# Where the first attention's keys are expanded, and when the gated layer's gates are copied

## What is computed

```python
x = x + tanh(g_xattn[0]) * retention(layernorm(x), ctx)      # decaying sum of k*v
x = x + tanh(g_ffn[0])   * moe(layernorm(x), 8 experts, top 2, gelu, hidden 512)
x = x + tanh(g_xattn[1]) * attention(layernorm(x), ctx)      # 16 heads of 8, rope, softmax
x = x + tanh(g_ffn[1])   * moe(layernorm(x), 8 experts, top 2, silu(a) * b, hidden 352)
x = x + tanh(g_xattn[2]) * additive attention(layernorm(x), ctx)   # tanh over all pairs
x = x + tanh(g_ffn[2])   * moe(layernorm(x), 16 experts, top 4, silu(a) * b, hidden 128)
x = x + tanh(g_xattn[3]) * attention(layernorm(x), ctx)
x = x + tanh(g_ffn[3])   * moe(layernorm(x), 8 routed experts and a shared one, top 2, gelu)
```

## Time and profile before

| | us |
|---|---|
| median of 3 runs | 616.18 (615.16 to 616.81) |
| the profiled execution | 613.41 |
| its span, first to last instruction | 611.6 |
| TensorE busy | 563.5 (92%) |
| VectorE busy | 445.4 (73%) |
| ScalarE busy | 415.8 (68%) |
| GpSimd busy | 117.0 (19%) |

### The profile page before, as it was taken

One profiled execution on the slowest core, in us unless ns is written; L12 is line 12 of the kernel. 1 busy time (PEld: TensorE's weight loads), 2 busy tenths in 40 slices (PEclk: granted clock), 3 DMA queues, 4 the chain that ended last, 5 costly groups with the idle time before them and its releaser, 6 DMA issues.

```text
span 611.6 us, 8766 instructions
## 1 busy us (share of the span) xinstructions
PE 563.5 (92%) x3281; PEld 390.9 (64%) x3284; DVE 445.4 (73%) x684; ACT 415.8 (68%) x581; POOL 117.0 (19%) x74
## 2 busy tenths in 40 slices
PE   7999999978998999998865899999998999999997
PEld 5667887846776777776210247556655777788886
DVE  4358988768646889986968658576767836787786
ACT  4779888916754565656999976624504856988885
POOL 5400000241210000002999914200000310000000
PEclk9999999979999999999899999999999999999999
DMA  6207110200200811020000022604610110812100
GB/s 233 70 15 298 49 55 1 73 2 1 75 1 3 312 38 41 34 69 1 2 5 1 1 69 70 194 16 122 190 34 1 38 36 0 297 50 70 35 1 34
DMA packets 16782, 40.27 MB, mean 66 GB/s; under 512 B 1834, under 2 KB 6058, under 8 KB 16740
## 3 DMA queue, kind: packets, MB, share of 16 engines
q1 hardware_dynamic: 16740, 39.71, 19.5%
HBM read 39.01 MB, written 0.70 MB: 65 GB/s over the span
## 4 chain that ended last, share of the span: by engine, by line
PE 71%; DVE 13%; ACT 11%; issue 3%; POOL 1%; ACTq 0%; DVEq 0%; POOLq 0%
PE ps L680 38%; ACT work L1046 7%; PE ps L723 4%; DVE h_lo L1523 3%; PE ps L445 2%; PE ps L573 2%; PE ps L706 2%; PE ps L544 2%; PE ps L708 2%; PE ps L707 2%; PE ps L462 2%; PE ps L662 2%; PE ps L558 2%; PE ps L452 2%; PE ps L439 1%
## 5 line engine op out<-in xcount | busy, mean ns | idle before, releaser
L1523 DVE TENSOR_TENSOR h_lo<-h_act,h_hi 128x512 fp32r<-128x512 f32 (+1 forms) x136 | 120.0, 886 | 41.0 <-ACT h_hi L1083 40.4
L680 PE MATMUL ps<-n_hi,w_hi 128*128 128x512 f32 (+1 forms) x232 | 85.8, 403 | 6.8 <-DVE h_act L1500 4.3
L1083 ACT CAST h_hi<-h_act 128x1024 fp32r<-128x1024 f32 (+1 forms) x88 | 75.3, 856 | 15.3 <-PE ps L680 12.8
L680 PE MATMUL ps<-n_hi,w_lo 128*128 128x512 f32 (+1 forms) x232 | 83.1, 392 | 0.0
L680 PE MATMUL ps<-n_lo,w_hi 128*128 128x512 f32 (+1 forms) x232 | 83.0, 391 | 0.0
L1721 POOL TENSOR_TENSOR rstd<-var_eps,minus_half 128x4 f32<-128x4 f32 x16 | 17.8, 1114 | 313.5 <-DVE var_eps L1217 313.5
L680 PE MATMUL ps<-h_hi,w_hi 128*128 128x512 f32 (+1 forms) x184 | 65.6, 399 | 4.5 <-DVE h_lo L1523 4.3
L680 PE MATMUL ps<-h_hi,w_lo 128*128 128x512 f32 (+1 forms) x184 | 64.3, 392 | 0.0
L680 PE MATMUL ps<-h_lo,w_hi 128*128 128x512 f32 (+1 forms) x184 | 64.0, 390 | 0.0
L1046 ACT ACTIVATE work<-work,p_rest 128x2048 f32<-128x2048 f32 x32 | 61.4, 2000 | 1.3 <-DVE work L1388 1.3
L1755 POOL TENSOR_TENSOR work<-xc,txt 128x2048 f32<-128x2048 f32 x16 | 58.3, 3684 | 5.0 <-ACT xc L1023 4.3
(11 more groups left out here) (225 smaller groups left out, 1015.9 us busy)
## 6 DMA issues: line engine op xcount, KB each, us to landing
work<-g_rows SPq DMA_DIRECT2D x36, 512.0 KB, 6.5
w_f<-in_w SPq DMA_DIRECT2D x20, 512.0 KB, 3.5
w_f<-in_w SPq DMA_DIRECT2D x8, 544.0 KB, 3.7
work<-in_w SPq DMA_DIRECT2D x2, 512.0 KB, 4.5
work<-g_rows SPq DMA_DIRECT2D x4, 256.0 KB, 9.2
p_rest<-in_p_rest SPq DMA_DIRECT2D x1, 714.0 KB, 9.9
p_attn<-in_p_attn SPq DMA_DIRECT2D x1, 546.5 KB, 7.0
x<-in_xT SPq DMA_DIRECT2D x1, 512.0 KB, 3.7
```

The lines of the kernel that those rows point to most:

```text
L680: mm = pe.matmul(dst[i], wap(wt, e, lo, size, rows), mv[i], start=(first and c == 0), stop=(last and c == 2))
L1083: act.copy(places(h_hi, m, step), places(h_act, m, step)).then_inc(s["hi"], 1)
L1523: dve.tensor_tensor(lo, src, hi.bitcast(F32), ALU.subtract).then_inc(s["lo"], 1)
```

## The change

ScalarE expands the first attention's keys in eight pieces (half `t`, head position `h`), each behind one of its steps 17, 19, 21, 23, 25, 27, 28 and 30 of the first expert layer; GpSimd's four expansions at the attention's start are gone. In the gated layer of 8 ScalarE copies the gates at step 7 and not at step 6, that is, behind the activation of step 7 and the cast of step 6, and behind the weight split of step 6.

```diff
-            def expand_keys(t, h):
-
-                act.wait_ge(pre["k"], 2 + t + 1)
-                low_ready(act, MOES[2], 15, "u")
-                src = kT[1][:, half(t)].rearrange("p (b k) -> p b k", k=S)
+            def expand_keys(i, t, h):
+
+                act.wait_ge(pre["k"], 2 * i + t + 1)
+                if i == 1:
+                    low_ready(act, MOES[2], 15, "u")
+                src = kT[i][:, half(t)].rearrange("p (b k) -> p b k", k=S)
                 ins = act.activation(kexp[:, 8 * t:8 * t + 8, h], src, ACT.Copy, scale=hmask[:, h:h + 1])
                 if h == 3:
                     ins.then_inc(at["kexp"], 2)
...
-                                    expand_keys(t, 2 * (step - 23 - 5 * t) + h)
+                                    expand_keys(1, t, 2 * (step - 23 - 5 * t) + h)
...
-                    if step == 6:
+                    if step == (7 if m.gated else 6):
                         copy_gates()
...
-            moe(MOES[0], {41: [lambda: norm_square(2, 0)], 42: [lambda: norm_copy(2, 0)], 43: [lambda: load_table(ACT.Exp)]})
+            heads = {step: [lambda t=t, h=h: expand_keys(0, t, h)] for t, steps in enumerate(((17, 19, 21, 23), (25, 27, 28, 30))) for h, step in enumerate(steps)}
+            moe(MOES[0], {**heads, 41: [lambda: norm_square(2, 0)], 42: [lambda: norm_copy(2, 0)], 43: [lambda: load_table(ACT.Exp)]})
...
-            def expand_keys(q):
-
-                src = kT[0][:, 4 * q * S:4 * (q + 1) * S].rearrange("p (b k) -> p b k", b=4)
-                pool.tensor_tensor(kexp[:, 4 * q:4 * q + 4], bcast(src, 2, 4), bcast(bcast(hmask, 2, S), 1, 4), ALU.mult).then_inc(at["kexp"], 1)
-
...
-            norm_power(2, 0)
-            pool.wait_ge(pre["k"], 2)
-            for q in range(2):
-                expand_keys(q)
-            norm_power(2, 1)
-            for q in range(2, 4):
-                expand_keys(q)
+            for t in range(2):
+                norm_power(2, t)
```

## The result

The changed kernel takes 606.95 us (median of 4, 606.25 to 608.30) against 615.67 us for the kernel before: a ratio of 0.9868 with an interval of 0.9843 to 0.9894, or 8.1 us less (6.5 to 9.7). Forecast were 610.4 us, 5.8 less than the 616.18 of that time, and a range down to 608.0.

A forecast was written before the change was run, and what follows sets the result against it. TensorE was taken to set the pace in both expert layers, so other engines' work counts only where TensorE waits. Terms -4.1 + 1.3 - 2.9 = -5.7 us against the median 616.18 gave 610.4 us, range 608.0 to 613.5.

The forecast's parts named there:

- (a): Hand-over to first attention: without GpSimd's expansions VectorE is undelayed and TensorE's h_lo wait goes; 4.1 us gained, bounds 2.0 to 4.6.
- the fall at the queries: First attention's start: TensorE's clock at 0.50 for 3.4 us was expected to stay at 1.00, gaining 1.7 us.
- half of 0.9: First attention's first scores: a second clock fall costing 0.9 us, given even odds of going, so counted at half.
- (b): First expert layer: ScalarE's eight added expansions, 4.9 us of work, were to cost 1.3 us, bounds 0 to 4.9.
- the instruction-by-instruction count of each pair: First expert layer, up to step 27: each ScalarE insertion leaves nearly 0.1 us lag per pair, some 0.55 us in all.
- the 0.1 us at steps 19 and 23: First expert layer: slack only about 0.7 us where VectorE's key rotation precedes h_lo, so 0.1 us counted lost.
- (c): Gated layer of 8: copying the gates at step 7 ends TensorE's wait behind their transpose; 2.9 us gained, bounds 2.0 to 2.99.
- R1: First attention's start: the clock stays low, the hand-over gains only 2.0 us, total 612.6 us; chance 0.15.
- R2: First expert layer: ScalarE becomes the bound, all 4.9 us of its expansions reach TensorE, total 614.1 us; chance 0.11.
- R3: Gated layer: the gates' wait only moves, to a gate's broadcast or a down; no gain there, total 613.4 us; chance 0.06.
- R4: Hand-over to first attention: VectorE's slowness has another cause than GpSimd, no gain there, total 614.6 us; chance 0.07.
- R5: First expert layer: ScalarE loads a table around each expansion, 20 us lost, total 629 us; chance 0.03.

The follow-up runs named there:

- GpSimd beside VectorE for nothing: Changed kernel plus two GpSimd expansions at the old place, into a tile nobody reads then: 610.70 us, ratio 0.9914.
- three further traces of before: The kernel before, run and profiled three more times with no edit: 616.94, 616.67 and 613.68 us.
- the keys alone: Changed kernel with the gates copied at step 6 again, so only ScalarE's key expansions differ from the kernel before: 612.57 us, ratio 0.9937.
- the filled stall: Kernel before plus eight constant-tile products on TensorE before the first expert layer's last down, where it waits for h_lo: 615.09 us, ratio 0.9984.
- The gates alone: Kernel before with only the gated layer's copy of the gates moved from step 6 to 7: 610.11 us, ratio 0.9912.
- filling the gates' pause: Kernel before plus twelve constant-tile products on TensorE behind the transpose of the gates, gates still at step 6: 613.62 us, ratio 0.9981.
- the early GpSimd variant: Changed kernel's gates, but GpSimd expands the keys, as soon as each half of the rotated keys is there: 611.22 us, ratio 0.9922.

## Why the prediction missed its range

**(a) GpSimd's expansions leave VectorE's way.** The mechanism was right and shown (GpSimd beside VectorE for nothing: 1.69, 2.27, 1.96 us). Size 4.1 forecast, 4.8 between the profiled executions: 2.2 for the wait (forecast 2.0), 1.55 for the fall at the queries (1.7), and 1.0 for what lies behind the fifth power, where I had put half of 0.9. Both falls went, by even odds for the second. Against the three further traces of before the whole is 2.3 to 3.5 us (54.8 to 56.0, less 52.5). The term "the 3.4 us at 0.50 hold the rest of the last `down` and the queries: 1.7 us gained" priced a fall that the three further traces of before don't have.

**(b) ScalarE's price.** This term was mis-sized: 0.8 us, not 1.3, in the changed kernel and by itself. The place was right, the wait for w_lo of expert 7. Two of my steps were too heavy. I took 0.1 us for the instruction-by-instruction count of each pair; in the trace an activation that starts late is followed by its cast 1.13 us later (70.54 and 71.67 on ScalarE's timeline), where I had used the 1.25 of the undisturbed ones (75.72 and 76.97). So the lag hardly grew from pair to pair: counted from the third power, the cast of step 28 comes 0.17 us later than before and the activation of step 29 0.80, where I had 0.6 and 1.2. And the 0.1 us at steps 19 and 23 was not there: TensorE has no other wait in that stretch.

**(c) The gates.** The failed step is here: I bounded the gain from above by the pause, 2.99 us, and put the clock behind it at nothing. Between the profiled executions it was 2.7 us, the remaining wait 0.18 against the 0.1 counted; that this agreed with the forecast is partly luck of the one profile, which had no fall there. But the pause costs more than its length in most executions, since the clock falls behind it: five of the six traces with the unfilled pause (three of before, the keys alone, the filled stall) have the fall, and the one without was the one I had. The gates alone gave 5.4 us, and the gated layer's gain against the three further traces is 4.3 to 5.6. I had even used the exception as evidence, in the sentence against R1 that "the gated layer's pause of 2.99 us in which the clock wasn't lowered ended with full-speed work, so not every pause is punished". One execution can't say that a pause is never punished.

**The sum against the median.** I noted that the profiled execution lay 2.8 us below the median and carried the gain over unchanged. That gap was itself a reading: the usual execution had something that the profiled one hadn't, and mean clocks say what. Of 51 executions of the kernel before beside these experiments, 43 had a mean clock of 0.983 or less; the profiled one had 0.988. The changed kernel's median lies 0.7 us above its profiled execution. The change removes two of the places at which executions differed, and so the gain is larger against the median than against a good execution. A part of the step is scatter of the three runs behind 616.18: the median of the 51 is 615.4. (By its own terms the sum is 616.18 - 5.7 = 610.5, not 610.4; that changes nothing.)

**The rivals.** R1 fell in the changed kernel's trace, though its question, when the clock falls, was the right one. R2: no, ScalarE's 4.9 us reached TensorE with 0.8. R3: no, the broadcast is 3.3 us early. R4: no, by the experiment. R5: no table load.

What stays open: why the clock falls in one execution and not in the next; whether the long fall at the start of the tanh is what made filling the gates' pause worth 1.2 and not some 2.5 us; and where the eight slower executions of the early GpSimd variant lost their time.

## What to carry to other kernels

A pause of TensorE in front of dense products costs its length and, in some executions, a fall of the clock behind it; one profile shows one draw of that. When the profiled execution is not near the median, ask first what the usual one has more, and read the mean clock of each. Look for a strictly ordered engine that stands in front of a wait with ready work behind it: moving the copy of the gates behind one activation was a single line and worth more than moving eight instructions between engines. Filling such a pause with idle products kept the clock in the one trace taken, but removing it gave over four times as much.

## What was unexpected of the hardware

The pause alone doesn't decide whether the clock falls. Behind the same 2.99 us of idleness TensorE ran on at 0.39 us per product in one execution and at 0.63 for nearly six microseconds in another, and behind 1.95 us of idleness the queries ran at full clock in one and at half in the other. The kernel before came out between 612.2 and 618.1 us in 51 executions, with mean clocks from 0.988 down to 0.974; by and large the slower ones had the lower clock.

A GpSimd instruction of 1.9 to 2.3 us with operands in SBUF held up a VectorE instruction with two operands in SBUF until 0.55 us behind its own end, whether or not anybody read its result: 0.69 us became 1.69 and 2.27.
